# Attention kernel: first projection piece moved inside step 0, first MLP layer issued by unit, copies of turned channels swapped, two load edits

## The reference

```python
x = x + L0(_gn(x))          # L0: full attention, 8 heads, 1024 x 1024 scores a head
x = x + L1(_gn(x))          # L1: layer norm over channels, windows, 4 sampled points a head
# L0
qkv = xs @ Wqkv + bqkv
scores = einsum('bhqd,bhkd->bhqk', q, k) / sqrt(64)
out = einsum('bhqk,bhkd->bhqd', softmax(scores), v)
out = out @ Wout + bout
# L1, a window: xn = layernorm(x) * ln_w + ln_b;  q = grouped 64x64 projection of xn
# offsets = 4 * tanh(pw @ gelu(depthwise conv(q)));  kv = bilinear samples of xn
# bias = W3 relu(W2 relu(W1 sign(pos) log1p|pos| + b1) + b2) + b3
# out = w_out @ (softmax(q k / 8 + bias) v) + b_out
```

## Time and profile before

| | us |
|---|---|
| median of 3 runs (lowest, highest) | 3527.37 (3524.6, 3533.67) |
| time of the profiled execution | 3524.64 |
| its span | 3522.8 |
| mean granted PE clock, share of full | 0.981 |
| PE busy | 3264.3 (93%) |
| DVE busy | 2216.4 (63%) |
| ACT busy | 1595.2 (45%) |
| 16 DMA engines, share of the span (queue 1) | 17.2% |

### The profile page before, as it was taken

One profiled execution on the slowest core, in us unless ns is written; L12 is line 12 of the kernel. 1 busy time (PEld: TensorE's weight loads), 2 busy tenths in 40 slices (PEclk: granted clock), 3 DMA queues, 4 the chain that ended last, 5 costly groups with the idle time before them and its releaser, 6 DMA issues.

```text
span 3522.8 us, 50334 instructions
## 1 busy us (share of the span) xinstructions
PE 3264.3 (93%) x20128; PEld 2160.1 (61%) x20128; DVE 2216.4 (63%) x2981; ACT 1595.2 (45%) x2322; POOL 220.9 (6%) x165
## 2 busy tenths in 40 slices
PE   6999798999989999899999999999999899987978
PEld 5766576556765567655776557765676555764544
DVE  5664567466666666676665856658567576655754
ACT  3541555264543555353552635426355263543533
POOL 0000020000100020000200002000020000200200
PEclk9999899999999999999999999999999999998979
DMA  4112012301123011311012111121112301103020
GB/s 172 30 52 71 16 33 70 103 25 35 33 70 101 31 37 33 99 64 43 26 57 92 46 48 33 56 93 45 38 33 77 103 19 40 34 10 101 24 56 36
DMA packets 142633, 192.21 MB, mean 55 GB/s; under 512 B 80897, under 2 KB 100868, under 8 KB 140836
## 3 DMA queue, kind: packets, MB, share of 16 engines
q1 hardware_dynamic: 142404, 188.99, 17.2%
HBM read 145.62 MB, written 43.32 MB: 54 GB/s over the span
## 4 chain that ended last, share of the span: by engine, by line
PE 80%; DVE 7%; ACT 4%; DMA 4%; issue 3%; SPq 1%; POOL 0%; DVEq 0%; ACTq 0%
PE banks L588 13%; PE banks L638 13%; PE banks L653 12%; PE banks L622 11%; PE banks L597 8%; PE banks L811 4%; PE banks L683 3%; PE banks L821 3%; PE banks L812 3%; PE banks L813 3%; ACT exps L1041 2%; DMA recips_dram<-recips 2%; DVE qk_halves L1487 2%; PE banks L882 2%; PE banks L786 2%
## 5 line engine op out<-in xcount | busy, mean ns | idle before, releaser
L1318 DVE TENSOR_REDUCE neg_max<-banks 128x1 f32<-128x1024 f32 x512 | 601.7, 1216 | 77.7 <-PE banks L622 75.9
L1041 ACT ACTIVATE exps<-banks,neg_max 128x1024 f32<-128x1024 f32 x512 | 564.9, 1111 | 176.7 <-DVE neg_max L1318 175.8
L1051 ACT ACTIVATE exps_turned<-banks 128x1024 f32<-128x1024 f32 x256 | 262.3, 1024 | 780.1 <-PE banks L638 780.1
L638 PE MATMUL banks<-ident,exps 128*128 128x128 f32 x4096 | 554.7, 279 | 56.6 <-ACT exps_turned L1051 43.3
L1327 DVE COPY exps_turned<-banks 128x1024 f32<-128x1024 f32 x256 | 313.3, 1224 | 455.8 <-PE banks L638 455.1
L638 PEld LDWEIGHTS banks<-ident,exps 128*128 128x128 f32 x4096 | 449.6, 141 | 212.6 <-issue 162.1
L653 PE MATMUL banks<-exps_turned,values 128*64 128x256 f32 x4096 | 473.3, 384 | 13.4 <-issue 8.2
L622 PE MATMUL banks<-qk_halves 64*128 64x512 f32 x3072 | 431.4, 412 | 58.3 <-ACT exps L1041 52.7
L653 PEld LDWEIGHTS banks<-exps_turned,values 128*64 128x64 f32 x4096 | 287.8, 137 | 162.7 <-issue 36.1
L622 PEld LDWEIGHTS banks<-qk_halves 64*128 64x128 f32 x3072 | 283.5, 187 | 145.5 <-issue 107.8
L597 PE MATMUL banks<-x_hi,wqk_ring 128*128 128x512 f32 x1024 | 350.2, 406 | 2.8 <-DMA wqk_ring<-wqk_split 2.8
(11 more groups left out here) (170 smaller groups left out, 3586.2 us busy)
## 6 DMA issues: line engine op xcount, KB each, us to landing
wqk_ring<-wqk_split SPq DMA_DIRECT2D x64, 512.0 KB, 4.0
recips_b<-recips_dram SPq DMA_DIRECT2D x256, 64.0 KB, 3.5
exps_turned<-in_x SPq DMA_DIRECT2D x32, 512.0 KB, 7.6
x_dram<-exps SPq DMA_DIRECT2D x32, 512.0 KB, 2.6
exps_turned<-x_dram SPq DMA_DIRECT2D x32, 512.0 KB, 5.7
out<-exps_turned SPq DMA_DIRECT2D x32, 512.0 KB, 2.6
x_image<-in_x SPq DMA_DIRECT2D x7, 2048.0 KB, 9.7
wv_halves<-wv_split SPq DMA_DIRECT2D x6, 2048.0 KB, 8.1
```

Source lines behind the costliest of these rows:

```text
L638: mm = pe.transpose(TB[:, kt // 4, kt % 4 * P:kt % 4 * P + P], PB[:, 2 * h + n % 2, kt * P:(kt + 1) * P], IDENT[:])
L1041: freed(act.activation(PB[:, 2 * h + n % 2], slot(("s", m, i)), ACT.Exp, bias=NM[:, m:m + 1], accum_out=SS[:, m:m + 1]), ("s", m, i))
L1318: dve.tensor_reduce(NM[:, m:m + 1], slot(("s", m, i)), AX.X, ALU.max, negate=True).then_inc(mx, 1)
```

## The change

1. `first_pair` of image 0 reads its weights from the split copies in SBUF and waits for the splits. The loads of pair 0 into the ring are gone, the two for pair 1 wait for nothing more, and the counts waited for on `wq_in` drop by one.
2. `WO0` is loaded after the fifteenth value product of an image and no longer after the sixteenth. The residual rows still wait for the sixteenth.
3. `piece(0, i)` moves on PE to between `turn(0, 0)` and `turn(0, 1)`, `high_piece(0)` on ACT behind the exponentials of step 1, and `low_piece(0)` on DVE behind the copy of the second turned half.
4. The first two units of the first MLP layer are issued one by one, each with its own wait, and the first two groups of `pixels` between and after them.
5. ACT copies the turned channels 1 and 3, DVE 0 and 2.

```diff
             def load_wq(c, i):
                 if c < 2 and i:
...
-                elif c in (2, 3):
+                elif c in (2, 3) and i:
                     wait_full(sp, ("q" if c == 2 else "k", 0, i))
...
-            load_wq(0, 0)
-            load_wq(1, 0)
             load_wq(2, 0)
             load_wq(3, 0)
...
+                sp.wait_ge(av_full, i * OUTS + OUTS - 1)
+                sp.dma_start(WO0, wo0.rearrange("(t p) n -> p t n", p=P)).then_inc(wo0_in, 16)
                 sp.wait_ge(av_full, i * OUTS + OUTS)
-                sp.dma_start(WO0, wo0.rearrange("(t p) n -> p t n", p=P)).then_inc(wo0_in, 16)
                 for t in range(CT):
                     sp.dma_start(XR[:, t], ...)
...
             def first_pair(w, i):
                 name = ("k" if w else "q", 0, i)
-                pe.wait_ge(wq_in[w], 16 * (PAIRS * i + 1))
+                if i:
+                    pe.wait_ge(wq_in[w], 16 * PAIRS * i)
+                else:
+                    pe.wait_ge(qk_split_hi, 2 * CT)
+                    pe.wait_ge(qk_split, 2 * CT)
                 wait_free(pe, name)
                 for c in (0, 512):
-                    mm = project_halves(slot(name)[:, c:c + 512], w, c, range(CT))
+                    mm = project_halves(slot(name)[:, c:c + 512], WQ[:, w] if i else (WQS, WKS)[w][:, 0], c, range(CT))
...
 (piece)
-                pe.wait_ge(wq_in[w], 16 * (PAIRS * i + p + 1))
+                pe.wait_ge(wq_in[w], 16 * (PAIRS * i + p))
...
 (mlp on PE)
+                def mlp1_unit(u):
+                    for w in range(2):
+                        rows = slice(32 * (2 * (u % 2) + w), 32 * (2 * (u % 2) + w) + 3 * ROWS)
+                        mm = pe.matmul(slot(("h1", u, j))[:, 512 * w:512 * w + 512], W1R[rows],
+                                       RR[rows, C * (u // 2):C * (u // 2) + C], start=True, stop=True)
+                    filled(mm, ("h1", u, j))
...
                 pe.wait_ge(rows_in[0], (j + 1) * 192)
-                mlp1(0)
+                for u in range(2):
+                    wait_free(pe, ("h1", u, j))
+                    mlp1_unit(u)
+                    if i is not None:
+                        pixels(u, i)
                 if i is not None:
-                    pixels(i)
+                    pixels(2, i)
+                    pixels(3, i)
                     pe.wait_ge(tpx_done[0], 2 * i)
...
 (PE, loop over images)
-                piece(0, i)
                 for n in range(STEPS):
                     if n + 1 < STEPS:
                         scores(n + 1, i)
                     turn(n, 0, i)
+                    if n == 0:
+                        piece(0, i)
...
 (ACT)
-                high_piece(0, i)
                 for n in range(STEPS):
...
                     copy_turned(n, i)      # and the exponentials of step n + 1
+                    if n == 0:
+                        high_piece(0, i)
...
-                for t in (0, 2):
+                for t in (1, 3):
                     wait_full(act, ("tc", t, i))
...
 (DVE)
-                low_piece(0, i)
                 for n in range(STEPS):
...
                     copy_turned(n, i)
+                    if n == 0:
+                        low_piece(0, i)
...
-                for t in (1, 3):
+                for t in (0, 2):
                     affine(t, i)
```

More of the change, by code:

```diff
@@ L592, in project, with project_halves @@
                 return mm
-            def project_halves(dst, w, c, ks):
+            def project_halves(dst, weights, c, ks):
                 for k in ks:
                     for a, half in ((0, XH), (0, XL), (1, XH)):
-                        mm = pe.matmul(dst, WQ[:, w, a, k], half[:, k, c:c + 512], start=(k == 0 and a == 0 and half is XH),
+                        mm = pe.matmul(dst, weights[:, a, k], half[:, k, c:c + 512], start=(k == 0 and a == 0 and half is XH),
                                        stop=(k == CT - 1 and a == 1))
@@ L664, in piece @@
                     pe.wait_ge(o1c_done, i - 1)
-                project_halves(MB, w, c, range(CT)).then_inc(piece_full, 1)
+                project_halves(MB, WQ[:, w], c, range(CT)).then_inc(piece_full, 1)
             def group_sums(k, dst, after=0):
@@ L752, in sampled_values, with pixels @@
                 mm.then_inc(vp_full, 1)
[L754 to L768, removed]
-                    if i:
-                        mm.then_inc(tpx_full[n % 2], 1)
-                    else:
-                        filled(mm, ("tp", n, i))
+            def pixels(n, i):
+                pe.wait_ge(gnorm_dve, 4 * i + n + 1)
+                pe.wait_ge(gnorm_act, 4 * i + n + 1)
+                if i:
+                    if n < 2:
+                        pe.wait_ge(gn_var, min(2 * i + 3, 2 * B))
+                    wait_after(pe, tpx_done[n % 2], 2 * (i - 1) + n // 2)
+                else:
+                    wait_free(pe, ("tp", n, i))
+                dst = (TB_ALL, OM_ALL)[n % 2] if i else slot(("tp", n, i))
+                for s in range(2):
+                    for t in range(CT):
+                        mm = pe.transpose(dst[:, 512 * s + P * t:512 * s + P * (t + 1)],
+                                          A[:, t, P * (2 * n + s):P * (2 * n + s + 1)], IDENT[:])
+                if i:
+                    mm.then_inc(tpx_full[n % 2], 1)
+                else:
+                    filled(mm, ("tp", n, i))
             def channel(t, i):
@@ L795, in mlp1 @@
                         wait_free(pe, ("h1", u, j))
-                    for s in range(4):
-                        u, w = 2 * v + s // 2, s % 2
-                        rows = slice(32 * s, 32 * s + 3 * ROWS)
-                        mm = pe.matmul(slot(("h1", u, j))[:, 512 * w:512 * w + 512], W1R[rows],
-                                       RR[rows, C * v:C * v + C], start=True, stop=True)
-                        if w:
-                            filled(mm, ("h1", u, j))
+                    for u in (2 * v, 2 * v + 1):
+                        mlp1_unit(u)
                 def mlp2(u, w):
@@ L977, in _ @@
                 else:
-                    pixels(i)
+                    for n in range(4):
+                        pixels(n, i)
                     first_pair(0, 1)
```

## The result

| | before | after |
|---|---|---|
| median of the runs, us | 3527.37 (3524.6 to 3533.67) | 3502.77 (3500.12 to 3509.41) |
| profiled execution: time, span | 3524.64, 3522.8 | 3505.46, 3503.7 |
| mean granted clock, profiled execution | 0.981 | 0.978 |

The ratio of the times is 0.9931 [0.9917, 0.9946], so the change takes 24.6 us off (19.0 to 29.3). It was predicted to take 29.3 off. Each kernel was run five times. The gains that the trace shows were larger than those in the sum, and stalls that the sum lacks took part of them back, so the nearness of the total is in part luck.

What follows compares the result with a forecast made beforehand. PE, busy 93% of the span, was taken as the bound. Terms 2.8 - 0.5 + 15.0 + 2.0 + 6.6 + 3.5 - 0.1 + 0 = 29.3 us, subtracted from 3527.37, gave 3498; range 3487 to 3512.

Steps and rivals of the forecast that it cites:

- A: Whole kernel: the forecast itself, 3498 us, own range 3490 to 3506; chance 0.68.
- B: Clock falls more at short waits left, step 0 of images 0 and 1 at half rate: 3510 us; chance 0.14.
- D: Output weights: the earlier `WO0` load pays as well, 8 to 11 us, giving 3488; chance 0.07.
- C: Images 2 to 7: step 0 does not pay, DVE's result or step 1 row maxima late: 3515 us; chance 0.06.
- Piece 0, images 2 to 7: Step 0: the moved piece fills two PE waits, 2.5 us in each of six images, 15.0, plus 2.0 for the clock.
- First layer by unit: First MLP layer, images 1 to 6: unit 0 and first pixels run during PE's wait, 1.1 us each, 6.6 gained.
- Swap: Turned-channel copies, images 1 to 7: `channel(2)` no longer waits, `channel(3)` starts sooner, 0.5 us each, 3.5 gained.
- `WO0`: Output-weight load: SP's own queue sets its time, so the earlier load gains 0; upper bound 11.8 us.
- Image 1: Step 0 of image 1: moved piece was already hidden; 0.5 us lost, between 0.4 gained and 4.0 lost.
- start and image 0: Start to `scores(2)` of image 0: 4.5 gained, less 0.2 for the piece and 1.5 for the clock, 2.8 us.
- both go: Start, `first_pair`: weights from SBUF remove the 2.81 us wait and 1.7 of low clock, 4.5 together.
- 1.5 by the price above, between 0 and 3 (two falls): Image 0, around `scores(0)`: longer PE pauses make a clock fall likely, costing 1.5 us, between 0 and 3.

Runs made afterwards that it cites:

- the three mends together: Kernel after, with DVE's copy ahead of its product, image 0's piece 0 in its old place, `WO0` ahead of SP's wait for the last store: 3502.23 us, 0.9862.

## Why the prediction was right, and where its terms were off

**Right.** 3498 was forecast and 3502.77 measured, by the mechanism named first. The waits named for the three largest terms are gone from the trace, or are down to the lengths named, and the largest term was tested alone. That the total came within 5 us is in part luck: the trace gains 31.6 at the places counted, and 10.9 more of stalls that the sum lacks stand against it. (The chances of A, B, D and half of C add to 0.92, and the prediction has 0.91; nothing hangs on it.)

- *Piece 0, images 2 to 7*: 15.0 and 2.0 for the clock were predicted; the trace has 15.4 (6.18 where 6.26 was worked out) and 3.1 (the falls of images 4 and 7 both gone). Alone, the edit takes 21 us off. Rival C falls: no wait is left in step 0, and the one of 0.6 ahead of `scores(3)` was there before.
- *First layer by unit*: 6.6 predicted, 7.5 in the trace, 6.0 in the time when alone.
- *Swap*: 3.5 predicted, 4.2 in the trace; `channel(3)` waits 0.5 as worked out.
- *`WO0`*: nothing predicted, 1.0001 alone. SP's queue was the reason: with the load ahead of SP's wait, PE's wait for it falls from 14.6 to 1.7.
- *Image 1*: 0.5 lost was predicted, 0.6 is gained in this trace. From `scores(1)` to `scores(2)` the eight traces with the moved piece have 7.59 to 8.67 and the six others 7.39 to 8.22, so the sign differs from one execution to the next; it hangs on how soon after `scores(1)` the clock comes back. To `scores(3)` the medians are 15.7 and 16.7. Nothing of size was lost there.

**The mis-sized term: start and image 0, 2.8.** Counted as the prediction does, from the end of the values to `scores(2)`, the trace has 29.90 before and 28.24 after, so 1.66. The edit alone shows 1.9 to 2.7 there, and nothing in the time. The wait of 2.81 is gone in every kernel with the new start. Two other steps failed.

The first is that with the weights in SBUF "both go", the wait and the 1.7 of low clock. The low clock stays and only moves. With the piece in its old place, each of the eight traces, of either start, has exactly one stretch of 3.4 us at the lower clock between the values and step 3: in `first_pair` in one, at `scores(0)` in five, at `scores(2)` in two.

The second is "1.5 by the price above, between 0 and 3 (two falls)". From `scores(0)` to `scores(2)` it is 14.53 after and 11.45 before: 3.1 lost, where 0.2 and 1.5 were counted. Both scores run slow, nearly the upper bound. In all four traces with the new start and the piece moved, one stretch of 10.2 us covers both; with the piece back in its old place, `scores(1)` takes 1.66. By the Trainium skill (TensorE: Matmul & The Clock Gate, HAM oscillation) a burst of matmuls behind a pause can start at the lower clock; this trace agrees, with a wait of 2.83 ahead of `scores(0)` and one of 3.72 ahead of `scores(1)`. With the old start and the piece moved the two traces differ (`scores(0)` takes 2.93 in one and 1.66 in the other), so which pause the fall meets is partly chance.

**A term that the sum lacks.** No edit touches DVE's product of line 1354, so the prediction left it out. PE's stalls from it were there before (the earlier trace rows do not show them, since 1.6 and 3.9 were the longest), and they are 10.9 us more in the trace after. The copy put first does not remove them: 41.9 in all, because the next value product waits for the same DVE product. Whether the change makes them likelier the runs don't settle. Their sum was 28.4 and 43.8 in two executions of the kernel after; in the first session 44.0 without the piece, 39.0 with the piece of image 0 in its old place and 28.6 with the piece alone; in the second, with one of the other edits alone, 15.4 to 25.3; in the third 31.5 with the start undone and 51.9 with `WO0` ahead of the wait. They go with the session at least as much as with the edit, and so does what DVE waits for. From the issue of a store of reciprocals to that of its load, 128 times a trace, the median is 8.4 to 8.6 us in the six traces of the first measurement and the second session, and 9.2 to 9.5 in the eight of the first and third sessions, which are also the slower ones. Why the way is longer there is open.

**The clock.** It was entered as a gain of 2.0, with rival B as its opposite, 3510. The falls of images 4 and 7 did go, but in the records the mean went from 0.981 to 0.978. B's mechanism, more falls at the short waits left, is not what the trace shows: 19 stretches for 20. Of the 21 us more at the lower clock, 17 stand at the three stalls of DVE's copy (20.5 for 3.4 at those places) and 6.8 in image 0 (10.2 for 3.4); the others grow and shrink and nearly cancel.

**Do the parts add?** The five edits alone have ratios of 0.9941, 0.9983, 0.9994, 1.0001 and 1.0004; their shortfalls add to 0.0077, and the whole change has 0.0069. The four without the piece add to 0.0018, and together they measured 0.0015. Within the intervals they add. Open are the 13.6 us of the undone start, and why the three mends together are worth 31.6 where 15 were expected. Their 15 held 5 for the copy put first, and the traces give that nothing (41.2 of waits for 43.8); the 13.5 of `WO0` are there. The kernel after ran at the lowest mean clock of that session (0.9755, the three others 0.977 to 0.979), so part of every difference against it is its clock. The late reciprocals differ between those traces too, and which of them drives the other was not tried.

## What to carry to other kernels

A piece of work pays where it fills a wait, and can lose where it filled one already: read the old place and the new one in every pass of the loop, the first passes by themselves. A load moved ahead of one wait gains nothing while its queue stands at another one before it; look at what that queue issues before the load. When an operation that waits for a DMA holds up a copy in an in-order queue, follow what that operation itself frees before reordering: here the bounding engine needed its bank next, and the wait only changed its name. Read the whole list of waits after such an edit, and not only the row that was to shrink.

## What the runs showed of the hardware

- The reciprocals' store of 2 KB to DRAM kept SP from the loads that need it for 6.8 to 14.1 us, with medians of 8.4 to 9.5 by trace. A load of 1 MB issued right behind the store made the last one of an image 1 us longer (means of 11.1 and 11.0 in two traces, 10.1 and 10.0 in the two others of that session). DVE's waits for the loaded values, in kernels that keep its order, vary from 46.0 (18 times) to 118.2 us (54 times) between traces.
- In the start, with the piece in its old place, one stretch of 3.4 us at the lower clock stood in each of eight traces, at one of three places; taking the wait of 2.81 away moved it and did not remove it.
- The kernel before had a median of 3524.5 in one session and 3549.02 in another on the same chip, with mean granted clocks of 0.9798 and 0.9771. In the kernels profiled in the slower session that keep DVE's order, DVE waited for reciprocals 49 to 57 times, in those of the faster session 18 to 21 times. Differences of under 1% need the kernel before beside them.
- Among the five runs of the kernel after, the longest had the lowest mean granted clock and the shortest the highest: 0.976 for 3509.41, 0.979 for 3500.12.
